# A graph layer and expert layer on one core: clock products, the order of the first loads, and who makes the normalized rows

## The reference

```python
deg = maximum((adj != 0).sum(-1), 1)
h = layernorm(x)
a_norm = rsqrt(deg) * (adj + I) * rsqrt(deg)      # deg is a column: each row is divided by its degree
x = x + relu((a_norm @ h + h) @ W + b)            # graph layer
h = layernorm(x)
logits = h @ gate_w.T                             # 8 experts, the best one, weight by softmax
y = sum over the chosen expert of comb * (silu(h @ w1.T) * (h @ w3.T)) @ w2.T
y = y + gelu(h @ sw1.T) @ sw2.T                   # shared expert, 1024 wide
x = x + y
```

## Time and profile before

| | us |
|---|---|
| median of 3 runs | 484.93 (484.72 to 486.24) |
| the profiled execution, its own time | 485.76 |
| its span | 484.2 |
| PE busy in the span | 448.4 (93%) |
| VectorE / ScalarE / GpSimd busy | 271.4 / 207.6 / 320.7 |
| mean granted clock of TensorE | 0.992 |

### The profile page before, as it was taken

How to read it: one execution, slowest core, us unless ns; L and a number is a source line. 1 busy time by engine, 2 the same in 40 slices (tenths; PEclk the granted TensorE clock), 3 DMA queues, 4 the chain that set the end, 5 groups by cost and what they waited for, 6 DMA issues and landing times.

```text
span 484.2 us, 8932 instructions
## 1 busy us (share of the span) xinstructions
PE 448.4 (93%) x2610; PEld 381.7 (79%) x2611; DVE 271.4 (56%) x557; ACT 207.6 (43%) x458; POOL 320.7 (66%) x293
## 2 busy tenths in 40 slices
PE   5999997999989999879988999999999999999992
PEld 4888775898869887768866888888888888888872
DVE  5875599655994499867774334333333433343330
ACT  3567584464545554474542332233222323232330
POOL 3457974376975799557896468966688579884112
PEclk9999998999999999999999999999999999999998
DMA  8466433302351055468576699997899562654000
GB/s 266 157 205 188 130 111 107 101 0 64 111 180 38 2 169 212 130 215 319 173 231 185 238 395 345 327 329 256 315 323 317 181 236 65 75 65 59 2 1 0
DMA packets 39612, 82.61 MB, mean 171 GB/s; under 512 B 5024, under 2 KB 14752, under 8 KB 37536
## 3 DMA queue, kind: packets, MB, share of 16 engines
q1 hardware_dynamic: 27024, 47.60, 30.1%
q0 software_dynamic: 7536, 29.39, 19.7%
q10 hardware_dynamic: 5024, 5.27, 3.7%
HBM read 74.74 MB, written 8.41 MB: 172 GB/s over the span
## 4 chain that ended last, share of the span: by engine, by line
PE 55%; DVE 10%; POOL 9%; issue 5%; SPq 2%; ACT 2%; DMA 2%; POOLq 0%; DVEq 0%; ACTq 0%
PE bank L1401 26%; PE bank L1428 9%; PE bank L1429 5%; PE bank L1320 4%; POOL a_lo L449 4%; PE bank L1414 4%; PE bank L1342 4%; DVE count L866 3%; POOL ering L492 2%; PE bank L1344 2%; DMA eraw<-in_experts 2%; POOL sorted_x L521 2%; POOL gel_lo L462 2%; DVE rows L821 1%; DVE rows L857 1%
## 5 line engine op out<-in xcount | busy, mean ns | idle before, releaser
L1401 PE MATMUL bank<-ering,xsT_hi 128*128 x368 | 121.5, 401 | 1.7 <-POOL ering L492 1.4
L449 POOL TENSOR_TENSOR a_lo<-araw,a_hi 128x512 fp32r<-128x512 f32 x64 | 94.6, 1496 | 40.1 <-ACT a_hi L612 39.4
L1222 PE MATMUL bank<-zz,a_hi 128*128 128x512 f32 (+1 forms) x256 | 95.1, 411 | 5.1 <-POOL a_lo L449 5.1
L1138 DVE SCALAR_TENSOR_TENSOR hid<-bank,xs,sil 128x512 f32<-128x512 f32 x46 | 34.5, 751 | 92.5 <-ACT sil L750 92.5
L1401 PEld LDWEIGHTS bank<-ering,xsT_hi 128*128 128x128 f32 x368 | 69.1, 188 | 18.1 <-issue 2.5
L1401 PE MATMUL bank<-ering,xsT_lo 128*128 x184 | 72.8, 396 | 0.0
L1224 PE MATMUL bank<-zz,a_lo 128*128 128x256 f32 (+1 forms) x256 | 72.5, 283 | 0.0
L750 ACT ACTIVATE sil<-bank 128x512 f32<-128x512 f32 x46 | 27.6, 599 | 101.6 <-PE bank L1401 101.6
L492 POOL TENSOR_TENSOR ering<-eraw,ering 128x512 fp32r<-128x512 f32 x40 | 51.7, 1314 | 28.8 <-DMA ering<-in_experts 20.7
L1428 PE MATMUL bank<-ering,hidT_hi 128*128 x184 | 67.1, 404 | 1.3 <-DVE hidT_lo L1146 1.3
L492 POOL TENSOR_TENSOR ering<-eraw_more,ering 128x512 fp32r<-128x512 f32 x48 | 60.7, 1299 | 8.4 <-PE bank L1180 4.3
(11 more groups left out here) (160 smaller groups left out, 826.4 us busy)
## 6 DMA issues: line engine op xcount, KB each, us to landing
araw<-in_adj_t SPq DMA_DIRECT2D x32, 512.0 KB, 4.1
eraw<-in_experts SPq DMA_DIRECT2D x48, 256.0 KB, 4.7
ering<-in_experts POOLq DMA_DIRECT2D x8, 1536.0 KB, 8.5
eraw_more<-in_experts SPq DMA_DIRECT2D x48, 256.0 KB, 5.9
ering<-in_experts POOLq DMA_DIRECT2D x8, 1024.0 KB, 6.6
ering<-in_experts POOLq DMA_DIRECT2D x8, 512.0 KB, 4.9
xs<-sorted_x ACTq DMA_DIRECT2D x20, 129.0 KB, 3.4
sw_raw<-in_sw_t ACTq DMA_DIRECT2D x2, 1024.0 KB, 5.4
```

The source lines that it names most:

```text
L449: pool.tensor_tensor(a_lo[:, u % AR, :], araw[:, u // CJ, u % CJ, :], a_hi[:, u % AR, :].bitcast(F32), ALU.subtract).then_inc(adj_lo_ok, 1)
L1222: pe.matmul(acc(q, it)[:, :], a_hi[:, s, it * P:(it + 1) * P], zt, start=first, stop=False)
L1401: ins = pe.matmul(bank[2 * w + h][:, :], a[:, k, :], ering[:, bass.ds(slot, 1), part, at:at + BANK].rearrange("p a n -> p (a n)"), start=n ...
```

## The change

- **Clock products**: they start after GpSimd's first constant (the identity), 18 of them instead of 10; 7 more follow the first transposes, 5 the first z product, 5 the first turn's transposes. PE's wait for the fourth constant goes ahead of `degrees(0)`.
- **Loads**: x's second group is issued ahead of the adjacency's first chunk; the bias goes out behind the split of W on ScalarE's queue.
- **First statistics**: tile 1's come ahead of `xn_low(0)`.
- **ScalarE's turn**: z_high, copy, xn_high, then (one turn later than before) the group's Sqrt, adj_high, and the row of t+3 last. VectorE makes `scales` a turn later, behind its z_low, xn_low and the bias sum.
- **Second norm**: in quarters 1 to 3 VectorE makes scale and shift alone, and ScalarE the four rows, two in turn 8 and two in turn 9. The last quarter's second norm stays with VectorE.
- **VectorE's order in the quarters**: the count of chunk 1 of quarter 1 goes ahead of the first degrees; shared pieces and counts are interleaved otherwise; in quarter 1 the gate's low part goes behind the last piece and the bias sum behind `xfT_lows`; in quarters 2 and 3 the bias sum follows the scales.

```diff
             rows_of_x(1, QT, x_loaded[0])
+            rows_of_x(QT, 2 * QT, x_loaded[1])
             for c in range(NC):
                 chunk(0, c, c if c >= RAW else None)
-                if c + 1 < NQ:
+                if 1 <= c < NQ - 1:
                     rows_of_x((c + 1) * QT, (c + 2) * QT, x_loaded[c + 1])
...
             act.dma_start(w_raw[:], w_in.rearrange("(k p) n -> p k n", p=P)).then_inc(w_loaded, 16)
-            act.dma_start(bias[:], b_in.rearrange("(a d) -> a d", a=1).partition_broadcast(P)
-                          ).then_inc(bias_loaded, 16)
...
             act.activation(w_hi[:], w_raw[:], ACT.Copy).then_inc(split_hi, 1)
+            act.dma_start(bias[:], b_in.rearrange("(a d) -> a d", a=1).partition_broadcast(P)
+                          ).then_inc(bias_loaded, 16)
             xn_high(0)
...
             for t in range(NT):
-                if QT <= t + 3 < NT:
-                    scaled_rows(t + 3)
                 z_high(t)
                 if t + 2 < NT:
                     xn_high(t + 2)
+                if t % QT == 1 and t // QT + 1 < NQ:
+                    stds(t // QT + 1)
                 adj_high(t % (RAW * CJ), t // (RAW * CJ) + 1, t - AR + 1 if t >= AR else None)
-                if t % QT == 0 and t // QT + 1 < NQ:
-                    stds(t // QT + 1)
+                if QT <= t + 3 < NT:
+                    scaled_rows(t + 3, (t + 3) // QT)
...
                     if j == AR + 3:
                         stds(NQ + q - 1)
+                    if AR + 4 <= j < AR + 6:
+                        for i in range(2):
+                            scaled_rows((q - 1) * QT + 2 * (j - AR - 4) + i, NQ + q - 1)
...
+            dve.wait_ge(x_loaded[0], 16)
+            statistics(group(0), 1, 2)
             xn_low(0)
-            dve.wait_ge(x_loaded[0], 16)
-            statistics(group(0), 1, QT)
+            statistics(group(0), 2, QT)
...
                     xn_low(t + 2)
+                if t < QT:
+                    z_and_bias(t)
+                if i == 1 and g < NQ:
+                    scales(g)
                 if i == 0 and g < NQ:
...
                     aggregates()
-                    scales(g)
...
+            count_chunks(1, 0, 2)
             inverse_degree(0)
-            count_chunks(1, 0, 1)
...
             for q in range(1, NQ):
-                count_chunks(q, 1 if q == 1 else 0, 2)
                 if q > 1:
+                    count_chunks(q, 0, 2)
                     dve.wait_ge(ln_ready, NT + (q - 1) * QT)
                 variances(group(q - 1))
                 count_chunks(q, 2, 3)
                 if q == 1:
-                    split_gate()
-                    shared_pieces(0, 2)
+                    shared_pieces(0, 1)
+                scales(NQ + q - 1)
+                if q == 1:
+                    shared_pieces(1, 3)
+                else:
+                    add_bias(q)
                 count_chunks(q, 3, RAW)
-                normalize(NQ + q - 1, group(q - 1))
-                add_bias(q)
                 if q == 1:
-                    shared_pieces(2, 4)
+                    shared_pieces(3, 5)
                 count_chunks(q, RAW, RAW + 1)
                 if q == 1:
-                    shared_pieces(4, 6)
+                    shared_pieces(5, 7)
                 count_chunks(q, RAW + 1, NC - 2)
                 if q == 1:
-                    shared_pieces(6, 8)
+                    shared_pieces(7, 8)
+                    split_gate()
                 xfT_lows(q - 1)
+                if q == 1:
+                    add_bias(q)
...
-            pe.wait_ge(consts, 4)
-            keep_clock_up(10)
+            pe.wait_ge(consts, 1)
+            keep_clock_up(18)
             xn_transpose(0)
+            keep_clock_up(7)
             pe.wait_ge(split_lo, 1)
             for t in range(NT):
                 z_tile(t)
                 if t == 0:
+                    keep_clock_up(5)
                     xn_transpose(1)
                 if t + 2 < NT:
                     xn_transpose(t + 2)
+                if t == 0:
+                    keep_clock_up(5)
...
+            pe.wait_ge(consts, 4)
             degrees(0)
```

More of the change, by code:

```diff
@@ L587, in stds, with scaled_rows @@
                                ).then_inc(std_ready, 1)
-            def scaled_rows(t):
-                act.wait_ge(scale_ready, t // QT)
+            def scaled_rows(t, k):
+                act.wait_ge(scale_ready, k)
                 act.activation(norm[:, t, :], resid[:, t, :], ACT.Identity, bias=shift[:, t % QT:t % QT + 1],
@@ L822, in normalize, with scales @@
                                       ALU.subtract, ALU.mult).then_inc(ln_ready, 1)
-            def scales(g):
-                dve.wait_ge(std_ready, g + 2)
-                dve.wait_ge(ln_ready, g * QT)
+            def scales(k):
+                dve.wait_ge(std_ready, k + 2)
+                dve.wait_ge(ln_ready, k * QT)
                 chained(dve.reciprocal(rstd[:], std[:]))
@@ L846, in z_low, with z_and_bias @@
                                   ALU.subtract).then_inc(z_ok, 1)
+            def z_and_bias(t):
                 if t == 0:
                     dve.wait_ge(bias_loaded, 16)
-                if t < QT:
-                    dve.tensor_tensor(norm[:, t, :], bank[6 + t % 2][:, 0:D], bias[:], ALU.add
-                                      ).then_inc(bias_added, 1)
+                dve.tensor_tensor(norm[:, t, :], bank[6 + t % 2][:, 0:D], bias[:], ALU.add).then_inc(bias_added, 1)
             def add_bias(q):
```

## The result

The changed kernel takes 481.73 us (median of 20 runs, 479.93 to 484.77) against 486.16 of the kernel before (20 runs of the same chips, 483.76 to 489.81): a ratio of 0.9915 [0.9896, 0.9933]. It is faster by 0.85%, about 4.1 us, where 9.1 were forecast; 481.7 lies outside 472.8 to 480.0. Of the 5.9 us between the forecast 475.8 and 481.7, 1.2 are the base alone: the forecast started from a median of three runs, 484.93, where twenty give 486.16.

A forecast was written before the change was run, and what follows sets the result against it. It took idle or slow PE time before 195 us as what the change could win. Front 2.2, second quarter 4.0, third and fourth 2.9 sum to 9.1: 485.76 to 476.7, less 0.83 for the median, 475.8; range 472.8 to 480.0.

The forecast's parts named there:

- Row 4: Front, ScalarE's first row, which PE awaits: starts at 14.4 instead of 14.62, a gain of 0.2 us.
- The bias: Front, bias load issued later on ScalarE's queue: lands near 10.9 when VectorE wants it, costing 0, up to 1 us.
- The clock: Front, PE's clock falls in a 2.7 us wait and returns near 18.5: 0 booked, 1.7 us either way as bounds.
- Steady front: Front's later turns: ScalarE's waits for aggregates and shift, and PE's two 1.0 us waits, vanish; 2.0 us gained.
- Second quarter: Second quarter: rows leave VectorE, ScalarE sets the pace, PE's stall near 77 and the half clock go; 4.0 us gained.
- The wait of 0.7 for the degrees: Second quarter's end: VectorE's remaining work ends near 84.5, so the degree products wait about 0.7 us.
- Third and fourth: Third and fourth quarters: PE's waits for counts ahead of the degree products go; 2 x 1.45 = 2.9 us gained.
- a_hi, a_lo run some 1 to 2 us ahead: Third and fourth quarters: that lead absorbs most of ScalarE's 2 us of rows; 0 to 0.5 us each comes back.
- What follows simply moves with it: From 195 us on: the chain of waits is bound to no absolute time, so it moves as a whole.
- Rows last holding up PE: Rival, front: rows at the end of ScalarE's turn come 1.0 us late in 12 turns; 489.8 us, chance 0.04.
- Part of the gain is eaten: Rival: second quarter's counts end 2 us later, or front's gain lost to late bias or clock; 478.3 to 479.8, chance 0.22.
- The clock did not hold: Rival, front: the clock holds over the 2.7 us wait, or the wait is shorter; 1.7 more, 474.1 us, chance 0.25.

The follow-up runs named there:

- Shift sooner: The changed kernel with the second group's scale and shift moved ahead of one bias sum on VectorE; ratio to the kernel before 0.9886.
- front alone: The kernel before with only the change's front: clock products, loads, first statistics, ScalarE's turn, scales a turn later; ratio to the kernel before 1.0027.
- count first: The changed kernel with the count of chunk 3 ahead of the bias sums in the third and fourth quarters; ratio to the kernel before 0.9913.
- no products: The changed kernel with the ten clock products of the kernel before in place of its 35; ratio to the kernel before 0.9902.
- bridge: The changed kernel with 24 more clock products in PE's wait for row 4; ratio to the kernel before 0.9869.
- three together: The changed kernel with bias issued behind W, second group's scales right behind its aggregates, chunk 3's count ahead of bias sums; 477.88 us, ratio to kernel before 0.9813.

## Why the prediction was wrong

Two terms of the sum failed: row 4 with the clock behind it, and the third and fourth quarters. Both have one reason in common: the forecast moved operations on VectorE and did not ask what GpSimd runs at their new time. Between the profiled executions 1.9 us were gained where 9.1 were forecast. The missing 7.2 are 3.2 in the front, 2.7 in the third and fourth quarters and 1.65 in the last stretch, less 0.4 that the second quarter gave on top.

- **Row 4, "a gain of 0.2 (bounds: +0.5, and -1.4 ...)": failed.** Measured -1.45; the bound of -1.4 stood for late clock products, which did not occur. The chain was counted with the shift at 0.16, as before (0.44 with the reciprocal). The same text let a shift cost "0.2 to 1.3" in the second quarter, where GpSimd was seen working, and did not ask what GpSimd does at 14.9: ScalarE has made an a_hi by then, so an a_lo starts there. Shift sooner showed the step at 1.27 us for 0.33 moved. The bias, "0, up to 1 us if the full queues slow it", was 0.70 late in the profiled run: its landing took 6.9 us and not 5.2, and it stands in the chain of work that ended last:

```profile
4.77 6.88 DMA bias<-in_gnn_b
```

  The 0.96 that the shift lost and these 0.70 are the whole way from the forecast 14.4 to 16.07. In four of the other kernels with the same late issue (front alone, count first, no products, bridge) VectorE did not wait for it; it is a risk of up to 0.8 us, not a constant.
- **The clock "to return where it did before, near 18.5".** It fell, as forecast, but the wait was 3.5 us and not 2.7, and it returned at 22.7 in after. PE was at work for 6.0 us of the low clock, which costs 3.0, against 1.7 before: 1.3 more where 0 was booked, near the bound of 1.7. In front alone it was the same; in count first, with the same 3.53 us of idle time, it was half as long: the granted clock of 12.9 to 55 us is 0.96 there and 0.92 in after, so 3.4 us against 6.7. So the extra loss is 0 or about 1.3 from one execution to the next of the same front.
- **Steady front, "both go, 2.0 us gained": right, net 1.5.** Both waits vanish; 0.21 and 0.26 for rows take their place, so the "margin of 0.1 to 0.4" was used up twice.
- **Second quarter, "4.0 gained (bounds 2.5 and 4.7)": right.** 4.36 between the marks, and by the pace given (1.6 and 2.7 us; measured 1.56 and 2.54). The wait of 0.7 for the degrees did not come.
- **Third and fourth, "2 x 1.45 = 2.9 (bounds 1.5 and 3.3)": failed.** Measured -0.38 + 0.59 = 0.2. The waits for counts did go, and 2.76 and 2.85 us were gained behind the last subtraction. The step that failed is "a_hi, a_lo run some 1 to 2 us ahead, so 0 to 0.5 each comes back": it looked at ScalarE's two us of rows and took GpSimd's pace as given. With the rows gone the counts run beside the subtractions, and the quarter's last twelve take 3.14 and 2.27 us longer. Count first brought 1.4 of the missing 2.7 back in the traces; there they still take 2.0 us longer than before (20.78 against 18.77 and 18.76), and the waits for a_lo that stay, 0.58 + 0.50 and 0.39 + 0.50 us against 0.31 and 0.32 before, are of the size of the rest. No run took the counts away from the subtractions altogether, so that last step rests on the traces. The forecast also overlooked that a count frees a place for a load (`sp.wait_ge(adj_counted, ...)` in `chunk`); ScalarE stood 3.78 and 4.67 us for it, but PE's waits for a_lo do not come from that.
- **"What follows simply moves with it".** Nearly: from 198 to about 258 the difference stays at 3.5 to 3.7 us, though the clock fell in after at 210.5 for 3.4 us: before waits 1.42 us for gel_lo at 217.83, and after does not. Then the clock fell once more at 258 in after's profiled run:

```profile
257.00:260.00 3.00, 1.99 (x5) 1.59 (x6) 2.11 (x5) 0.28 (x1) 1.29 (x2) 0.71 0.81 243
```

  A spell of 3.4 us at half costs 1.7 us, which is the 1.65 of the last stretch. Such spells come after waits of 1 to 3 us near 208 and 258 in some executions of several kernels here; the runs do not say what decides it.
- **Rivals.** Rows last holding up PE (489.8) is refuted: 0.21 and 0.26 us twice, not 1.0 twelve times. "Part of the gain is eaten" (478.3 to 479.8) was the nearest in kind. It named the front's gain lost to a late bias or clock, and counts beside a working GpSimd, but these in the second quarter alone and with the price on the counts, not on the subtractions; and its 2.5 to 4 us were less than the 5 that went. The clock did not hold.
- **The Trainium skill.** "SBUF — State Buffer", section SBUF: two separate sides, was used for a rival alone. By its rule a shift with two SBUF inputs that meets an a_lo waits until that one ends; here the trace agrees to 0.02 us (1.12 us of shift, both ending at 16.0). Applied to every VectorE operation in the changed chain it would have priced row 4 at 1.0 later. The counts, which the prediction called mixed, agree too where they stand beside subtractions: by turns, 1.08 and 1.15 us behind each other's end, and the price falls on both engines. "TensorE: Matmul & The Clock Gate", Part 1, on cold products that vary from run to run: the runs agree, as far as 3.4 and 6.8 us at half for one front go; the range had room for it.

## What to carry to other kernels

When an operation is moved on VectorE, look up what GpSimd runs at its new time, not at its old one: a 0.16 us operation on [128 x 4] can cost 1.1. When work leaves VectorE, what stood behind it comes earlier: look up what that will stand beside, and price both engines, as the counts cost GpSimd 3.1 us in one quarter. A long wait, such as ScalarE's 3.78 us for a load, is a cause only if the next engine in the chain stood idle for it; GpSimd had not. And clock products belong into the longest idle time, not ahead of it: 25 more before it were worth nothing as long as it was 3.5 us, 24 in it some 2 to 3 us.

## What the runs showed of the hardware

- The size of an operation does not shield it. A SCALAR_TENSOR_TENSOR of 128x4 took 0.16 us alone and 1.12 beside a GpSimd subtraction of 1.26, in six kernels, and always until that one's end. The reciprocal of the same size, with one input, took 0.16 to 0.18 us in these turns.
- The same idle time can let the clock fall or not: after 2.06 us it held in three together and fell in two others, at once or 0.9 us later. In front alone 2.53 us at 77.6 left it up (granted clock 1.00 from 76 to 77), where 2.48 had let it fall before; it fell there behind the next wait, 2.28 us at 82.4 (0.66 from 83 to 88, 3.4 us at half). Around 260 us PE waited 1.36 us before and 1.37 in after; the clock held in the first and fell in the second. The spells of half clock seen here lasted 3.4 or 6.8 us each, the one that the end of a trace cuts off aside.
- A count (SCALAR_TENSOR_TENSOR of 128x1024) and a GpSimd subtraction of 128x512 take turns. Alone they take 1.2 and 1.3 us, side by side 2.1 and 2.3, each ending 1.1 to 1.2 behind the other. Where both start within 0.01 us, as in count first at 117.59, the one that was first takes its usual 1.21 and the other 2.35.
- So VectorE's counts became slower as they moved: 28 of them average 1773 ns, by the groups by line, where the same groups show 1504 before. That is 28 x 0.27 = 7.5 us, more than half of the 14.2 us of rows that left VectorE (17.1 us in 20 rows before, 2.9 in 8 after). GpSimd's 64 subtractions average 1608 ns, against 1496.
